# Layer 1 attention: from a loop over pairs of tiles to four unrolled chunks of four tiles

## The reference, cut to what matters

```python
h = h + _L1_attn_ref(_layernorm(h, axis=-1), L1_attn_Wq, L1_attn_bq, L1_attn_Wk, L1_attn_bk, L1_attn_Wv, L1_attn_bv)

def _L1_attn_ref(Z, Wq, bq, Wk, bk, Wv, bv):
    D = Z.shape[-1]
    scale = 1.0 / D ** 0.5
    Q = jnp.einsum('bsd,ed->bse', Z, Wq) + bq
    K = jnp.einsum('bsd,ed->bse', Z, Wk) + bk
    V = jnp.einsum('bsd,ed->bse', Z, Wv) + bv
    scores = jnp.einsum('bqd,bkd->bqk', Q, K) * scale
    attn = jax.nn.softmax(scores, axis=-1)
    Z_hat = jnp.einsum('bqk,bkd->bqd', attn, V)
    return Z_hat
```

## Time and profile before

| what | us |
|---|---|
| median of 3 executions (2767.41 to 2771.04) | 2768.43 |
| span of the profiled execution, first to last instruction | 2760.7 |
| attention block of layer 1, from POOL's first copy to the end of the last L1278 | 553.4 to 635.5 |
| normalise before it: last record of L371 begins; normalise after it: first record of L297 | 551.8; 636.1 |
| PE busy in the whole span | 2111.9 (76%) |
| DVE busy in the whole span | 1301.2 (47%) |
| ACT busy in the whole span | 895.0 (32%) |

### The profile page before, as it was taken

How to read it: one execution, slowest core, us unless ns; L and a number is a source line. 1 busy time by engine, 2 the same in 40 slices (tenths; PEclk the granted TensorE clock), 3 DMA queues, 4 the chain that set the end, 5 groups by cost and what they waited for, 6 DMA issues and landing times. The chain is left out here.

```text
span 2760.7 us, 45402 instructions
## 1 busy us (share of the span) xinstructions
PE 2111.9 (76%) x13260; PEld 1494.0 (54%) x13260; DVE 1301.2 (47%) x2968; ACT 895.0 (32%) x1852; POOL 729.3 (26%) x728
## 2 busy tenths in 40 slices
PE   9746777884974994977899647776579953999998
PEld 9412224573753883654467312222469843989987
DVE  4349983324554113553112679999522236222222
ACT  1247862222341332332112455554222211221111
POOL 0004540002010452000000027776023421344343
PEclk9658996785885996996899769999689965999999
DMA  7000000000003771000210000000067714777774
GB/s 210 15 0 1 0 0 1 0 0 6 1 0 87 196 205 35 1 0 0 61 58 18 0 0 1 0 0 0 23 199 217 218 30 132 214 220 223 226 202 126
DMA packets 77891, 201.83 MB, mean 73 GB/s; under 512 B 17718, under 2 KB 47289, under 8 KB 69465
## 3 DMA queue, kind: packets, MB, share of 16 engines
q1 hardware_dynamic: 52760, 169.74, 18.7%
q0 software_dynamic: 25056, 31.22, 6.9%
HBM read 179.25 MB, written 22.91 MB: 73 GB/s over the span
## 5 line engine op out<-in xcount | busy, mean ns | idle before, releaser
L1742 POOL DMA_INDIRECT sums<-yblock,put x129 | 206.0, 1597 | 422.5 <-DVE yblock L2005 316.2
L1995 DVE TENSOR_TENSOR hid<-sa,banks 128x512 f32<-128x512 f32 (+1 forms) x183 | 105.9, 579 | 353.1 <-ACT sa L1882 218.4
L1790 PE MATMUL banks<-xTblock,wt 128*128 128x256 f32 (+1 forms) x1464 | 267.9, 340 | 1.9 <-ACT xTblock L1861 1.5
L1815 PE MATMUL banks<-wt,hid 128*128 128x192 f32 x1548 | 268.5, 327 | 0.1
L1882 ACT ACTIVATE sa<-banks 128x512 f32<-128x512 f32 (+1 forms) x183 | 93.2, 509 | 488.2 <-PE banks L1801 449.0
L1815 PEld LDWEIGHTS banks<-wt,hid 128*128 128x128 f32 x1548 | 249.2, 190 | 3.8 <-DVE hid L1995 3.0
L1790 PEld LDWEIGHTS banks<-xTblock,wt 128*128 128x128 f32 x1464 | 235.4, 193 | 24.8 <-issue 1.9
L632 PE MATMUL banks<-g,consts 128*128 128x400 f32 x384 | 184.7, 571 | 60.2 <-DVE g L771 56.2
L740 POOL TENSOR_TENSOR w<-u,spreadB 128x400 f32<-128x400 f32 x192 | 192.9, 1037 | 86.9 <-ACT spreadB L711 86.9
L371 PE MATMUL banks<-consts,xs 100*96 100x100 f32 (+1 forms) x320 | 72.8, 384 | 172.4 <-DVE xs L322 132.9
L1737 POOL DMA_INDIRECT xblock<-table,take x135 | 134.5, 997 | 224.1 <-DVE put L1971 114.2
(11 more groups left out here) (397 smaller groups left out, 3767.8 us busy)
## 6 DMA issues: line engine op xcount, KB each, us to landing
wt<-L3f_packed SPq DMA_DIRECT2D x41, 1152.0 KB, 5.6
wt<-L3f_packed SPq DMA_DIRECT2D x41, 576.0 KB
wt<-L3m_packed SPq DMA_DIRECT2D x20, 1152.0 KB, 5.5
wt<-L_packed SPq DMA_DIRECT2D x20, 579.0 KB
wt<-L3m_packed SPq DMA_DIRECT2D x20, 577.0 KB
wt<-L_packed SPq DMA_DIRECT2D x20, 576.0 KB
pixels<-pixels SPq DMA_DIRECT2D x16, 375.0 KB, 4.0
wu<-L_up SPq DMA_DIRECT2D x8, 576.0 KB, 4.8
```

The lines of the kernel that those rows point to most:

```text
L1742: nc.gpsimd.indirect_dma_start(t.sums, bass.IndirectOffsetOnAxis(put[:, q:q + 1], 0), y[:, b % 2, q - column_of_block[b], :], None, comput ...
L1790: nc.tensor.matmul(bank[:, n * j:n * (j + 1)], wt[:, v, cols(base, 2 * p + j)], xT[:, v, 0, 0:n], start=(j == 0), stop=False, skip_group_c ...
L1815: last = nc.tensor.matmul(bankY[s], hid[:, m, 128 * s:128 * (s + 1)], wt[:, v, DOWN_AT + DIM * m:DOWN_AT + DIM * (m + 1)], start=(m == 0 a ...
L1995: nc.vector.tensor_tensor(hid[:, 2 * p:2 * p + 2, 0:n], sa[:, (PAIRS * v + p) % 2, 0:2 * n].rearrange("p (m n) -> p m n", m=2), second[:, ...
```

## The change

The block is rewritten without loops, as four chunks (c) of four tiles (j), with functions that are called in a written order.

- POOL's stream and the tile `x` are gone. The products read `t.xT` straight: the queries and keys (L1210 of the new program) stream 400 columns, one chunk, and each m has a PSUM bank of its own; the values (L1220) take slices of 100 from `t.xT` as weights.
- Queries are taken from PSUM by ACT (L1275), keys by DVE (L1300), 400 columns each. Values are taken two tiles at a time (L1307).
- The four tiles' scores lie in one bank (L1233). DVE scales and masks them with one instruction (L1313) and reduces them with one (L1316). The exponentials stay four instructions (L1285). The turned probabilities of a chunk are taken with one instruction (L1291), the reciprocals with one (L1320). The additions to `t.h` stay one for each tile (L1325).
- PE's order for chunk c is: scores, the products m = 0, 1, 2 of the next chunk, the transposes, the product m = 3 of the next chunk, the outputs, and then the values of the next chunk, which write the banks that the outputs had and so wait for `added`.

The diff, with removed lines left out where the new ones take their place in another form:

```diff
@@ layer1_mixer @@
-        x = t.sbuf("xtile", [HALF + 1, 2, 2, TILE], st)
-        qk = t.sbuf("qk", [HALF, 2, 4, TILE], st)
...
-        bankP, bankV, bankS = t.bank[0:2], t.bank[2:4], t.bank[4:6]
+        qk = t.sbuf("qk", [HALF, 2, 4, CHUNK], st)
+        v_ = t.sbuf("v", [TILE, 2, 4, DIM], st)
+        s = t.sbuf("scores", [TILE, 4, TILE], st)
+        p = t.sbuf("probs", [TILE, 4, TILE], st)
+        pT = t.sbuf("probsT", [TILE, 4, TILE], st)
+        low, tot, inv = (t.sbuf(n, [TILE, 2, 4], st) for n in ("low", "tot", "inv"))
+        names = ("projected", "qk_done", "qk_done_too", "values_up", "v_done", "scored", "masked", "low_done", "exp_done", "turned", "pT_done", "out_done",
+                 "inv_done", "added")
+        (projected, qk_done, qk_done_too, values_up, v_done, scored, masked, low_done, exp_done, turned, pT_done, out_done,
+         inv_done, added) = (t.sem(n) for n in names)
+        bankP, bankV, bankS, bankT = t.bank[0:4], t.bank[4:6], t.bank[6], t.bank[7]
+        fours = lambda bank: bank[0:TILE, 0:4 * TILE].rearrange("p (j n) -> p j n", j=4)
-            @block.gpsimd
-            def _(pool):
-                with pool.Fori(0, TILES // 2) as i:
-                    for u in range(2):
-                        pool.wait_ge(projected, 2 * i + u + 1)
-                        pool.sem_inc(t.passed, 1)
-                        nc.gpsimd.tensor_copy(x[:, u], t.xT[0:HALF + 1, :, bass.ds(TILE * (2 * i + u), TILE)]).then_inc(staged, 1)
...
+                def project_qk(c, m):
+                    if c:
+                        if m < 2:
+                            pe.wait_ge(qk_done, 2 * (c - 1) + m + 1)
+                        else:
+                            pe.wait_ge(qk_done_too, 2 * (c - 1) + m - 1)
+                    at = slice(CHUNK * c, CHUNK * (c + 1))
+                    for k, depth in enumerate((HALF + 1, HALF)):
+                        last = nc.tensor.matmul(bankP[m][0:HALF, 0:CHUNK], w["L1_wqk"][0:depth, k, HALF * m:HALF * (m + 1)], t.xT[0:depth, k, at],
+                                                start=(k == 0), stop=(k == 1))
+                    last.then_inc(projected, 1)
+
+                def project_v(c):
+                    if c:
+                        pe.wait_ge(added, 4 * c)
+                    for j in range(4):
+                        at = slice(CHUNK * c + TILE * j, CHUNK * c + TILE * (j + 1))
+                        for k, depth in enumerate((HALF + 1, HALF)):
+                            last = nc.tensor.matmul(bankV[j // 2][0:TILE, DIM * (j % 2):DIM * (j % 2 + 1)], t.xT[0:depth, k, at], w["L1_wv"][0:depth, k, :],
+                                                    start=(k == 0), stop=(k == 1))
+                        if j % 2:
+                            last.then_inc(values_up, 1)
+
+                def score(c):
+                    pe.wait_ge(qk_done, 2 * c + 2)
+                    pe.wait_ge(qk_done_too, 2 * c + 2)
+                    if c:
+                        pe.wait_ge(masked, c)
+                    for j in range(4):
+                        at = slice(TILE * j, TILE * (j + 1))
+                            last = nc.tensor.matmul(bankS[0:TILE, at], qk[:, c % 2, k, at], qk[:, c % 2, 2 + k, at], start=(k == 0), stop=(k == 1))
+                    last.then_inc(scored, 1)
+
+                def turn_(c):
+                    if c:
+                        pe.wait_ge(pT_done, c)
+                    for j in range(4):
+                        pe.wait_ge(exp_done, 4 * c + j + 1)
+                        last = nc.tensor.transpose(bankT[0:TILE, TILE * j:TILE * (j + 1)], p[:, j, :], w["ident"][0:TILE, 0:TILE])
+                    last.then_inc(turned, 1)
+
+                def output(c):
+                    pe.wait_ge(pT_done, c + 1)
+                    pe.wait_ge(v_done, 2 * c + 2)
+                    for j in range(4):
+                        nc.tensor.matmul(bankV[j // 2][0:TILE, DIM * (j % 2):DIM * (j % 2 + 1)], pT[:, j, :], v_[:, c % 2, j, :],
+
+                for m in range(4):
+                    project_qk(0, m)
+                project_v(0)
+                for c in range(CHUNKS):
+                    score(c)
+                    if c + 1 < CHUNKS:
+                        for m in range(3):
+                            project_qk(c + 1, m)
+                    turn_(c)
+                    if c + 1 < CHUNKS:
+                        project_qk(c + 1, 3)
+                    output(c)
+                    if c + 1 < CHUNKS:
+                        project_v(c + 1)
+
+                def take_qk(c):
+                    for m in range(2):
+                        act.wait_ge(projected, 4 * c + m + 1)
+                        if c >= 2 and m == 0:
+                            act.wait_ge(scored, c - 1)
+                        nc.scalar.activation(qk[:, c % 2, m, :], bankP[m][0:HALF, 0:CHUNK], ACT.Identity).then_inc(qk_done, 1)
+
+                take_qk(0)
+                for c in range(CHUNKS):
+                    act.wait_ge(low_done, c + 1)
+                    if c:
+                        act.wait_ge(turned, c)
+                    if c >= 2:
+                        act.wait_ge(inv_done, c - 1)
+                    for j in range(4):
+                        nc.scalar.activation(p[:, j, :], s[:, j, :], ACT.Exp, bias=low[:, c % 2, j:j + 1], accum_out=tot[:, c % 2, j:j + 1]).then_inc(exp_done, 1)
+                    if c + 1 < CHUNKS:
+                        take_qk(c + 1)
+                    act.wait_ge(turned, c + 1)
+                    if c:
+                        act.wait_ge(out_done, 4 * c)
+                    nc.scalar.activation(pT[:], fours(bankT), ACT.Identity).then_inc(pT_done, 1)
+                def take_k(c):
+                    for m in range(2, 4):
+                        dve.wait_ge(projected, 4 * c + m + 1)
+                        if c >= 2 and m == 2:
+                            dve.wait_ge(scored, c - 1)
+                        nc.vector.tensor_copy(qk[:, c % 2, m, :], bankP[m][0:HALF, 0:CHUNK]).then_inc(qk_done_too, 1)
+
+                def take_v(c):
+                    for i in range(2):
+                        dve.wait_ge(values_up, 2 * c + i + 1)
+                        if c >= 2 and i == 0:
+                            dve.wait_ge(out_done, 4 * (c - 1))
+                        nc.vector.tensor_copy(v_[:, c % 2, 2 * i:2 * i + 2, :], bankV[i][0:TILE, 0:2 * DIM].rearrange("p (j d) -> p j d", j=2)).then_inc(v_done, 1)
+
+                def highest(c):
+                    dve.wait_ge(scored, c + 1)
+                    if c:
+                        dve.wait_ge(exp_done, 4 * c)
+                    nc.vector.scalar_tensor_tensor(s[:], fours(bankS), DIM ** -0.5, w["mask"].unsqueeze(1).to_broadcast([TILE, 4, TILE]),
+                                                   ALU.mult, ALU.add).then_inc(masked, 1)
+                    dve.wait_ge(masked, c + 1)
+                    nc.vector.tensor_reduce(low[:, c % 2, :], s[:], AX.X, ALU.max, negate=True).then_inc(low_done, 1)
+
+                def finish(c):
+                    dve.wait_ge(exp_done, 4 * c + 4)
+                    nc.vector.reciprocal(inv[:, c % 2, :], tot[:, c % 2, :]).then_inc(inv_done, 1)
+                    dve.wait_ge(inv_done, c + 1)
+                    for j in range(4):
+                        dve.wait_ge(out_done, 4 * c + 4 if j >= 2 else 4 * c + 2)
+                        tile = t.h[:, 4 * c + j, :]
+                        nc.vector.scalar_tensor_tensor(tile, bankV[j // 2][0:TILE, DIM * (j % 2):DIM * (j % 2 + 1)], inv[:, c % 2, j:j + 1],
+
+                take_k(0)
+                take_v(0)
+                for c in range(CHUNKS):
+                    highest(c)
+                    if c + 1 < CHUNKS:
+                        take_k(c + 1)
+                    finish(c)
+                    if c + 1 < CHUNKS:
+                        take_v(c + 1)
```

More of the change, by code:

```diff
@@ L1186, in layer1_mixer @@
     with ExitStack() as st:
-        x = t.sbuf("xtile", [HALF + 1, 2, 2, TILE], st)
-        qk = t.sbuf("qk", [HALF, 2, 4, TILE], st)
-        v_ = t.sbuf("v", [TILE, 2, DIM], st)
-        s = t.sbuf("scores", [TILE, 2, TILE], st)
-        p = t.sbuf("probs", [TILE, 2, TILE], st)
-        pT = t.sbuf("probsT", [TILE, 2, TILE], st)
-        low, tot = t.sbuf("low", [TILE, 2], st), t.sbuf("tot", [TILE, 2], st)
-        inv = t.sbuf("inv", [TILE, 2], st)
-        staged, projected, qk_done, v_done, scored, masked, low_done, exp_done, turned, pT_done, out_done, inv_done, added = (
-            t.sem(n) for n in ("staged", "projected", "qk_done", "v_done", "scored", "masked", "low_done", "exp_done",
-                               "turned", "pT_done", "out_done", "inv_done", "added"))
@@ L1241, in _ @@
                 nc.scalar.preload_act_table(ACT.Exp)
-                with act.Fori(0, TILES // 2) as i:
-                    n = lambda u: 2 * i + u + 1
-                    for u in range(2):
```

(34 more changed lines are left out.)

26 lines of the change are left out of this document (removed).

## The result

| | us |
|---|---|
| kernel before, first four executions | 2762.69 to 2771.04, median 2767.92 |
| changed kernel, four executions | 2729.58 to 2734.34, median 2732.35 |
| ratio of the two | 0.987, 95% interval 0.9846 to 0.9894 |
| changed kernel again, beside 19 new executions of the kernel before | 2731.82 against 2761.22, ratio 0.9887 (0.9864 to 0.9909) |
| and once more, beside 7 others | 2735.28 against 2760.16, ratio 0.9907 (0.9891 to 0.9924) |

The change gains 35.6 us by the first comparison, 29.4 and 24.9 by the later two. One of the 12 executions of the kernel before in experiment 1 took 3752.79 us, at a mean granted clock of 0.577 where the other eleven have 0.838 to 0.844, and is left out of every number here. I had forecast 27.1 and written 2741; the measured time lies outside the range of 2736 to 2750.

What follows compares the result with a forecast made beforehand. PE was taken to bound the block, through idle gaps and a falling clock. Start to 563.25, three periods of 36.75 and a last chunk of 8.3 gave a 27.1 us gain: 2768.4 - 27.1 = 2741.3 us, range 2736 to 2750.

Steps and rivals of the forecast that it cites:

- What bounds the stage: Old block: PE, idle 15.6 us in a chain two tiles cannot fill, with its mean granted clock at 0.83.
- rival 1: New block: clock falls in every period, each half-clock stretch costing 1.65 us; 2743 to 2748 us, chance 0.24.
- The streams at full clock: PE's products: 0.34 us per 400-column pass against 4 x 0.085 for four narrow ones; width change counted as nothing.
- The period: New block, scores of one chunk to the next: 12.25 us, PE idle 1.25; three periods add 36.75 us.
- the new wait: PE, before the next chunk's values: waits for all four additions, 1.25 us per chunk.
- The start: First projection and values: 8.0 us at full clock plus 1.95 for half clock, upper end 2.9; reaches 563.25.
- The last chunk: Block's end, softmax uncovered: 7.7 us, or 8.9 with outputs at half clock; middle 8.3 taken, ending at 608.3.
- The block as a whole: Rewritten block: ends at 608.3 where it ended at 635.45, a gain of 27.1 us.
- (2): New block: clock stays at half throughout, 96.3 us against the old 82.1; slower, 2783 us, chance 0.03.
- (3): New block: stalls no row shows, such as code waits or longer DVE chain; 2749 to 2757 us, chance 0.06.
- (4): PE's wide passes cheaper than their columns: 64 passes would save 11.5 us, 2730 us, chance 0.02.
- (5): Whole block: the change does nothing because the stage is hidden behind something else; chance 0.01.

Runs made afterwards that it cites:

- experiment 1: Kernel before and changed kernel both run again, unchanged: kernel before median 2762.42 us over eleven executions, 2761.22 over 19; changed kernel 2731.82 us.
- Experiment 4: Kernel before, with unread products of 400 columns behind the scores and 200 behind the outputs, where PE stood idle: 2750.21 us, ratio 0.9964.
- experiment 3: The padded kernel: kernel before with 25 one-element memsets on DVE at the block's start, shifting its later code: 2758.39 us, ratio 0.9988.

## Why the prediction was right and wrong

**What bounds the stage** was right: one chain with gaps, and a clock that falls behind the gaps. Experiment 4 puts 11.5 us on the clock (1.65 for each fall were read from the earlier trace rows for rival 1, and there were seven) and 15.1 on the gaps.

**The streams at full clock** were right. A wide pass takes 0.34; the width as such brings 0.7 us where I had counted nothing.

**The period** was summed at 12.25 and is 12.22. Its parts: masking 0.57 (taken 0.57 between 0.26 and 0.63), reduction 0.57, the softmax covered with 1 us to spare, the new wait 1.16 for 1.25, and no other wait of PE. That the masking came out to the hundredth was luck, and without weight: under the cover either bound gives the same period.

**The start**: from the first product (553.74) to the first scores (564.23) are 10.5 us where I had 9.95. The granted clock was 0.50 until 558.6 and 0.83 in the next 0.2 us, so it cost 2.5 us where I took 1.95. The upper end of 2.9 goes 0.2 beyond what the earlier trace rows give (2.7), and was not reached.

**The last chunk** was summed at 8.3 us, the middle of 7.7 and 8.9. The outputs ran at half clock, which was the upper bound's case, and it took 8.7 us, from the scores at 600.87 to the end of the last additions at 609.61.

**The block as a whole**: 27.1 us forecast, 26.5 measured.

**The step that failed** is the one after the sum: "The median of the timed executions is 7.7 us above that span, the part around it; I leave that as it is". The part around a span is 1.8 us. The other 5.9 were the distance between one quick execution and the median of three, and I carried them over to the new kernel as if they were fixed. From the profiled execution's own time, 2762.5 - 27.1 gives 2735.4 us. That would still have been 3 us above 2732.35. Of this 1.0 us is a term that the sum did not have: it speaks of the code of the block and nowhere of the code behind it, whose place gave that much in layer 3 (experiment 3). The other 2 us are less than the scatter, and stay open. And the range allowed 3.6 us "for the spread of executions", from three of them, where 19 have a spread of 21 us and one loop far from the change swings by 12.

**The rivals**: the clock does not fall in the periods (rival 1) and does not stay at half (2); no product of PE in the block waits without a releaser (3); wide passes cost their columns (4); the change acts in full (5).

## What to carry to other kernels

Sum a change against the time of the execution that was profiled, and ask for the scatter before writing a range: three executions do not show it. Compare traces by stretches between landmarks that both programs have; here that gives 0.05 us for the block, where medians give 5. But ask of each stretch what its clock was before crediting a change: the padded kernel's 416.3 us agreed with the changed kernel's for another reason. And when a chain with gaps is to be filled, price the gap twice, once for the idle time and once for the clock behind it; if the gap can't be filled with work, a product that nobody reads brings the second part.

## What the runs showed of the hardware that I had not expected

- A loop of DVE that no edit touched ran 1.0 us slower or faster in four trips, by where its code lay: four pauses of 0.25 us that the profile calls "issue" (experiment 3). The Trainium skill (Runtime: NRT & Kernel Launch, Instruction fetch mechanics) says that a taken branch whose target is outside the held window has to fetch it first. The pauses at the three turns of a short loop, and their going with a shift of 25 instructions, are in keeping with that; the fourth, inside the first trip, is at no taken branch, and no run here shows a fetch.
- Products that nobody reads shorten a program: 11.5 us in the old loop, 2.4 and 1.3 us at the ends of the new block.
- One loop of layer 2 took from 166.6 to 178.4 us in twelve traces, with the granted clock from 0.86 to 0.79 in its windows, and this is the largest part of the scatter: no other stretch that was left alone differs by more than 7 us over the twelve.
